# Query transfers, normalisation's end, local stage and both ends moved; dense products between global scores in a one-core transformer mixer layer

## What is computed

```python
xn = layernorm(x)
# attention: 16 heads of 16; 4 global (causal), 12 local (causal, 64 back)
q, k, v = split(xn @ w_qkv + b_qkv)
ctx = softmax(mask(q @ k.T * 0.25)) @ v
attn = ctx @ w_out + b_out
# two branches of 8 experts of rank 64, on Q, K and on Q @ W_inv.T, K @ W_inv.T
prod = (Q @ V) * cumsum(K @ W)
weights = softmax(gelu(Q @ router_w1.T + router_b1) @ router_w2.T + router_b2 + expert_bias)
branch = ((prod * weights) @ U + weights @ b) / position
ffn = (fwd + alpha * inv) @ W_O.T
out = x + attn + ffn
```

## Time and profile before

| | us |
|---|---|
| median of 3 runs | 1456.86 (1455.05 to 1458.92) |
| the profiled execution: its own time | 1456.11 |
| its span, first to last instruction | 1454.4 |
| TensorE busy (matmul) | 1356.6 (93%) |
| VectorE busy | 1012.4 (70%) |
| ScalarE busy | 774.1 (53%) |
| GpSimd busy | 581.9 (40%) |

### The profile page before, as it was taken

One profiled execution on the slowest core, in us unless ns is written; L12 is line 12 of the kernel. 1 busy time (PEld: TensorE's weight loads), 2 busy tenths in 40 slices (PEclk: granted clock), 3 DMA queues, 4 the chain that ended last, 5 costly groups with the idle time before them and its releaser, 6 DMA issues.

```text
span 1454.4 us, 35948 instructions
## 1 busy us (share of the span) xinstructions
PE 1356.6 (93%) x14481; PEld 1031.0 (71%) x14481; DVE 1012.4 (70%) x2082; ACT 774.1 (53%) x1368; POOL 581.9 (40%) x663
## 2 busy tenths in 40 slices
PE   5888999999999999999999999999999999999986
PEld 4567685777858777686867868587775878678773
DVE  6667877568756887568775777567885678757661
ACT  3334537464564636655374644647356463845544
POOL 2034343453424444354434535254442534345350
PEclk9999999999999999999999999999999999999997
DMA  8530625416172542617253171624517163441710
GB/s 184 126 95 23 168 69 136 116 60 175 41 170 69 128 128 73 153 32 179 76 129 110 57 188 29 170 83 110 146 43 181 34 154 102 118 121 42 185 34 16
DMA packets 184279, 154.45 MB, mean 106 GB/s; under 512 B 37554, under 2 KB 183857, under 8 KB 184113
## 3 DMA queue, kind: packets, MB, share of 16 engines
q1 hardware_dynamic: 184112, 152.16, 40.8%
HBM read 108.57 MB, written 37.22 MB: 100 GB/s over the span
## 4 chain that ended last, share of the span: by engine, by line
PE 66%; DVE 10%; ACT 8%; issue 6%; DMA 5%; POOL 3%; SPq 2%; ACTq 0%; POOLq 0%; DVEq 0%
PE PS L699 34%; PE PS L811 11%; PE PS L847 4%; ACT HE L1092 3%; PE PS L906 3%; PE PS L892 3%; DMA rest<-weights_d 2%; ACT HE L1084 2%; PE PS L924 2%; PE PS L833 2%; PE PS L989 2%; PE PS L935 2%; DMA weights_d<-weights_t 2%; PE PS L867 2%; DVE tok L1191 1%
## 5 line engine op out<-in xcount | busy, mean ns | idle before, releaser
L1540 POOL TENSOR_TENSOR PL<-prod,PH 128x512 fp32r<-128x512 f32 x128 | 167.4, 1308 | 180.6 <-ACT PH L1066 180.3
L1535 POOL TENSOR_TENSOR prod<-prod,rest 128x512 f32<-128x512 f32 x96 | 123.2, 1283 | 263.5 <-DMA rest<-weights_d 183.0
L1066 ACT ACTIVATE PH<-prod 128x512 fp32r<-128x512 f32 x128 | 80.8, 631 | 264.4 <-DVE prod L1340 264.4
L699 PE MATMUL PS<-XH,WH 128*128 128x512 f32 x512 | 216.9, 424 | 4.5 <-DVE rest L1209 1.8
L1264 DVE TENSOR_REDUCE block_peak<-PS 128x4 f32<-128x512 f32 x288 | 179.8, 685 | 49.0 <-PE PS L847 48.9
L699 PE MATMUL PS<-XH,WL 128*128 128x512 f32 x512 | 203.4, 397 | 0.0
L699 PE MATMUL PS<-XL,WH 128*128 128x512 f32 x512 | 203.1, 397 | 0.0
L1092 ACT ACTIVATE HE<-PS 128x512 f32<-128x512 f32 (+1 forms) x320 | 159.9, 552 | 34.3 <-PE PS L906 31.4
L1517 POOL TENSOR_SCALAR_AFFINE_SELECT HE<-HE 128x256 f32<-128x256 f32 x128 | 51.2, 406 | 287.2 <-ACT HE L1092 283.7
L1340 DVE TENSOR_TENSOR prod<-PS,prod 128x512 f32<-128x512 f32 x128 | 87.7, 685 | 94.5 <-PE PS L699 73.1
L811 PE MATMUL PS<-UH,PH 128*128 128x256 f32 x512 | 134.9, 296 | 0.0
(11 more groups left out here) (190 smaller groups left out, 3046.2 us busy)
## 6 DMA issues: line engine op xcount, KB each, us to landing
parts_d<-area SPq DMA_DIRECT2D x32, 768.0 KB, 5.0
area<-parts_d SPq DMA_DIRECT2D x128, 192.0 KB, 5.9
rest<-weights_d SPq DMA_DIRECT2D x192, 128.0 KB, 3.6
area<-parts_d SPq DMA_DIRECT2D x32, 576.0 KB, 5.7
tok<-in_L_attn_x_dram SPq DMA_DIRECT2D x16, 512.0 KB, 6.2
xt<-in_L_attn_x_dram SPq DMA_DIRECT2D x16, 512.0 KB, 4.7
wide<-weights_d SPq DMA_DIRECT2D x64, 128.0 KB, 3.5
out_dram<-xt SPq DMA_DIRECT2D x16, 512.0 KB, 4.1
```

Of the source, the lines that this page charges most:

```text
L699: ins = e.matmul(ps, a, b, start=first and k == 0, stop=last and k == n - 1, skip_group_check=True)
L1066: e.activation(PH[:, h, :], prod[:, j % 3, :], ACT.Copy).then_inc(phi)
L1535: e.tensor_tensor(prod[:, j % 3, :], prod[:, j % 3, :], wide[j % WIDE], ALU.mult).then_inc(weighed)
L1540: e.tensor_tensor(PL[:, j % 2, :], prod[:, j % 3, :], PH[:, j % 2, :].bitcast(F32), ALU.subtract).then_inc(plo)
```

## The change

All of it is in the order of the stages, in who does two sets of memsets, and in how one stage is cut:

- **Dense between scores.** In a global block the side work now stands between the first and the second score (in the last block behind both), and then comes the `gav` of the block before. `norm` pieces are hung on the value groups.
- **Local stage.** Both `turn`s come ahead of the first scores; `parts` start one group earlier; `hidden 0` moves into the sixth group.
- **Norm's end in parts.** "scale" is no longer a piece of `norm`: it is four stages of one operation each, behind peak blocks 2 to 5 (for chunk 1: all four behind the last peak group). `tok_done` counts four per chunk.
- **Query transfers.** The four are cut 3 + 1 around the transfer of `wide 0`, in place of 2 + 2.
- **Both ends.** `consts`' memsets of SBUF go into `boot`, the first stage, still on DVE. `settle` moves from DVE to POOL, with its waits. In the last chunk the expert work left over starts behind the first local group, and `finish` 15 0 stands in the middle of the global stage, not behind its first block.

```diff
-    NORM = (... "correct", "square", "correct", "scale")
+    NORM = (... "correct", "square", "correct")
...
     def global_groups(ch):
-        order = []
         tl = tiles(ch % NC)
-        for n, (j, half) in enumerate(tl):
-            order.append([(add_gscore, ch, j, half, pair) for pair in range(2)])
-            if n:
-                order.append([(add_gav, ch, *tl[n - 1])])
-        return order + [[(add_gav, ch, *tl[-1])]]
+        scores = [[[(add_gscore, ch, j, half, pair)] for pair in range(2)] for j, half in tl]
+        return scores, [[(add_gav, ch, j, half)] for j, half in tl]
...
         if ch == 0:
             add_norm(1, order)
+            for t in range(T):
+                order[-1].append((add, "scale", 1, t))
...
         run(experts[0] + peaks[0])
         if ch and nxt:
-            add("norm", ch + 1, len(NORM) - 1)
+            for t in range(T):
+                peaks[2 + t].append((add, "scale", ch + 1, t))
         weave(experts[1:split], peaks[1:])
...
         if nxt:
-            side = [[(add_turn, ch + 1, 0), (add_turn, ch + 1, 1)] + last_mix, [(add_rows, ch, 1)]]
-            side += [[(add_parts, ch + 1, w, b)] for w in (1, 0) for b in range(DB)]
-            side[-1] += [(add, "sums", ch + 1, k) for k in range(DB)]
+            for k in range(DB):
+                add_turn(ch + 1, k)
+            side = [last_mix] + [[(add_parts, ch + 1, w, b)] for w in (1, 0) for b in range(DB)]
+            side[1].append((add_rows, ch, 1))
+            side += [[(add_hidden, ch + 1, 0)] + [(add, "sums", ch + 1, k) for k in range(DB)]]
...
-            side = [[(add_rows, ch, 1)]] + experts[split:] + [last_mix]
+            side = experts[split:] + [last_mix]
+            side[0] = side[0] + [(add_rows, ch, 1)]
         weave(local_groups(ch), side)
...
-            for j in range(2 * DB):
+            for j in range(1, 2 * DB):
                 add_hidden(ch + 1, j)
...
+        last, done = len(scores) - 1, 0
+        for n in range(1, last + 1):
+            upto = -(-len(side) * n // last)
+            between = [stage for group in side[done:upto] for stage in group]
+            done = upto
+            first, second = scores[n]
+            run(first + (second + between if n == last else between + second) + values[n - 1])
+        run(values[last])
...
@@ vector_program, "boot" (moved here from "consts")
+                    for c in range(NC):
+                        e.memset(block_peak[c][:, :, :, :], LOWEST)
+                    q.step(e.memset(peak[:, :, :], 0.0))
+                    for view, value in ((ones1, 1.0), (wslots[:, :, :], 0.0), (Va[:, :, :, :], 1.0)):
+                        ins = e.memset(view, value)
+                    ins.then_inc(readied)
...
@@ vector_program
-                    else:
-                        for t in range(T):
-                            ins = e.tensor_scalar(tok[:, t, :], tok[:, t, :], mv[:, t, 0:1], var[:, 3, t:t + 1], ALU.subtract, ALU.mult)
-                        ins.then_inc(tok_done)
+                elif kind == "scale":
+                    ch, t = key
+                    q.wait_step()
+                    e.tensor_scalar(tok[:, t, :], tok[:, t, :], mv[:, t, 0:1], var[:, 3, t:t + 1], ALU.subtract, ALU.mult).then_inc(tok_done)
...
@@ gpsimd_program (in vector_program it had no waits, and is gone there)
+                elif kind == "settle":
+                    q.wait_ge(fold_ps, product_nth("fold", 5, 1))
+                    q.wait_ge(out_lo, 1)
+                    for view in (WT[G16:KSTK, :], KL[G16:KSTK, :, WINDOW:], KG[G16:KSTK, :, :]):
+                        e.memset(view, 1.0).then_inc(ones_set)
+                    q.wait_ge(ones_set, 3)
...
@@ sync_program, "stacks"
-                        for rows, i in STACK if half is None else STACK[2 * half:2 * half + 2]:
+                        for rows, i in STACK if half is None else (STACK[:3], STACK[3:])[half]:
```

More of the change, by code:

```diff
@@ L151, in peak_use @@
         return f"bank{(4, 5, 6, 7)[turns['peak'] % 4]}"
-    NORM = ("moments", "start", "square", "correct", "square", "correct", "square", "correct", "scale")
+    NORM = ("moments", "start", "square", "correct", "square", "correct", "square", "correct")
     def add_lpeak(ch, t, grp, bank):
@@ L322, in add_norm @@
         at_ = len(order) // 3
-        steps = len(NORM) - (1 if ch > 1 else 0)
-        for n in range(steps):
-            order[at_ + n * (len(order) - at_) // steps].append((add, "norm", ch, n))
+        for n in range(len(NORM)):
+            order[at_ + n * (len(order) - at_) // len(NORM)].append((add, "norm", ch, n))
     def peak_groups(ch):
@@ L352, in mixer_layer @@
         add("norm", 0, n)
+    for t in range(T):
+        add("scale", 0, t)
     add("split_qkv")
@@ L434, in mixer_layer @@
             add("stacks", ch + 1, "local")
-            for j in range(2 * DB):
+            for j in range(1, 2 * DB):
                 add_hidden(ch + 1, j)
-        order = global_groups(ch)
-        side = []
+        scores, values = global_groups(ch)
         if nxt:
             first_x, first_c = ([(add, ch + 1, 0, part) for part in range(2)] for add in (add_x, add_c))
-            run(first_x + order[0] + first_c)
+            run(first_x + scores[0][0] + scores[0][1] + first_c)
             add("logits", ch + 1, uses=["bank7"])
             add("chigh", ch, 0)
-            order = order[1:]
             if ch + 2 < CHUNKS:
[L447 to L450, removed]
+                add_norm(ch + 2, values)
+            side = [[(add_gates, ch + 1), (add, "crest", ch, 0)], [(add_gate_parts, ch + 1)]] + [[]] * (2 * (ch % NC))
+            side += [[(add_values, ch + 1, 0)], [(add_values, ch + 1, 1)], [(add_finish, ch, 0)]]
         else:
+            run(scores[0][0] + scores[0][1])
             add("crest", ch, 0)
-        side.append([(add_finish, ch, 0)])
-        weave(order, side)
+            side = [[], [(add_finish, ch, 0)]]
+        last, done = len(scores) - 1, 0
[6 more added lines that the diff above has]
+        run(values[last])
         if nxt:
@@ L713, in tensor_program @@
                         q.wait_ge(selected, 2)
-                    q.wait_ge(tok_done, ch + 1)
+                    q.wait_ge(tok_done, T * (ch + 1))
                     take(i, *stage)
@@ L1168, in vector_program @@
                         q.wait_ge(x_in, 16 * (ch + 1))
-                        q.wait_ge(tok_done, ch)
+                        q.wait_ge(tok_done, T * ch)
                         for t in range(T):
@@ L1233, in vector_program @@
                     e.tensor_tensor(p3, left, p2, ALU.subtract).then_inc(part3)
-                elif kind == "settle":
-                    for view in (KL[G16:KSTK, :, WINDOW:], KG[G16:KSTK, :, :], WT[G16:KSTK, :]):
-                        e.memset(view, 1.0).then_inc(ones_set)
                 elif kind == "keep":
@@ L1387, in vector_program @@
                 elif kind == "consts":
-                    for c in range(NC):
-                        e.memset(block_peak[c][:, :, :, :], LOWEST)
-                    q.step(e.memset(peak[:, :, :], 0.0))
-                    for view, value in ((ones1, 1.0), (wslots[:, :, :], 0.0), (Va[:, :, :, :], 1.0)):
-                        ins = e.memset(view, value)
-                    ins.then_inc(readied)
                     q.wait_ge(selected, N_SELECT)
```

## The result

| | before | changed |
|---|---|---|
| median of the runs, us | 1457.89 (4 runs, 1455.05 to 1462.80) | 1439.14 (4 runs, 1437.22 to 1442.25) |
| profiled execution: own time, span | 1456.11, 1454.4 | 1440.78, 1439.1 |
| PE, DVE, ACT, POOL busy | 1356.6, 1012.4, 774.1, 581.9 | 1354.2, 987.6, 773.4, 595.0 |

The ratio is 0.9869, with a 95% interval of 0.9844 to 0.9894: 1.3% faster, 15.3 us between the two spans. The lines of the changed kernel stand 9 to 13 lines further down: L776 is now L785, L833 is L842, L867 is L876, L699 is L708; the scalings' L1191 is L1208.

A forecast was written before the change was run, and what follows sets the result against it. PE was taken as the bound, computing 1356.6 of 1454.4 us, with many small waits left to win. The terms summed to -24.0, taking 1456.1 to 1432, with a range of 1420 to 1447.

The forecast's parts named there:

- right: Success signs: POOL's memsets 9 to 14 us; PE waits: L1077's mask under 4 us, `open` under 5, queries under 4.
- wrong: Failure signs: new PE waits for DVE in odd chunks; global scores waiting for exps over 15 us; query wait unchanged.
- `consts`, -1.7: Start: memsets move into DVE's idle time in `boot`, PE's 2.52 us wait partly won; bounds 0 and -2.5.
- `settle`, -2.8: Start: memsets leave DVE for POOL, PE's 3.04 us wait for the gate transpose falls; bounds -2.2 and -3.0.
- Chunk 0, -1.0: Four scalings come behind `found`, taking 1.38 us for 2.49 ahead of a product PE awaits; bounds 0 and -3.1.
- Local stage, -6: Dense work in the second group covers mask waits of 9.6 us; 0.4 us in 15 chunks; bounds 0 and -9.6.
- Odd front, -9: Gates-to-`open` chain: 1.05 us sooner in 8 chunks (-8.4), scalings -2.5, landing against issue +1.9; bounds -2.5 and -18.5.
- the third query ahead of `wide` 0 costs 0: Odd front: it would push `wide` 0 back by 0.3 us, covered by PE's 1.04 us of waiting; size 0.
- Scalings, -2.5 and +1.5 in the peak blocks: -2.5: 0.5 us in each of five odd fronts; +1.5: scalings delaying maxima or products, 0.2 us in seven odd chunks.
- the port rival: Odd chunks: each of 28 scalings meets a POOL multiplication, 21 us come back, no change at 1453; chance 0.07.
- Dense between scores, 0: Global blocks: first exp over early, second exp behind the `Va` copy; 0 net, bounds -4 and +6.
- Last chunk, -5: Last chunk: -3.5 from local-stage waits and slower clock, -1.5 from `finish` leaving the global front; bounds -2 and -8.

The follow-up runs named there:

- e8: e2 with the raw weights of `w_out` and U on two semaphores, and chunk 1's four scalings behind product 6 of chunk 0: 1430.69 us, ratio 0.9798.
- e5: Kernel before with the scalings' part of the change alone, four single operations behind peak blocks: 1444.45 us, ratio 0.9900.
- e12: Kernel before with the query transfers cut 3 + 1 around `wide` 0, nothing else: 1461.43 us, ratio 1.0020.
- e6: e2 with one step moved on VectorE alone, the transposition `ctx` 2 ahead of the queries' first `parts`: 1429.34 us, ratio 0.9793.
- e3: Changed kernel with `hidden` 0 back behind the local stage, all else kept: 1452.26 us, ratio 0.9964.
- e7: e2 with turns behind the first two scores, `mix` 7 split over two groups, `parts` and `hidden` 0 as before the change: 1436.56 us, ratio 0.9841.
- e2: Changed kernel with the query transfers cut 2 + 2 around `wide` 0, as before the change: 1431.40 us, ratio 0.9821.
- e4: Changed kernel with the old order of the global stage, `finish` 15 0 left in the middle: 1443.45 us, ratio 0.9887.
- e1: Changed kernel with the four scalings back in one set ahead of the expert stage, chunk 0's kept behind `found`: 1452.72 us, ratio 0.9953.

## Why the prediction was right, and which steps were not

It said 1432.0 with 1420 to 1447; the runs say 1439.1. In spans it was 24.0 to win, and 15.3 were won. Sign and range held, but not for the reasons given. Of its own signs, no wait at `open`, 0.2 us for L1077's masks and 9.2 us of memsets came as "right" had them; the wait for the queries came to 4.9 us, not under 4, and the new waits for products in odd chunks (3.7) were on its list for "wrong".

- **`consts`, -1.7: measured -0.4.** The 2.52 us went, and 2.56 for the last raw weights came, at 36.85 (before 37.23). The term let the second transfer land 4.6 us after its issue near 30.7, at 35.4; the chain that ended last has it under way for 6.0 (start us, us):

```profile
30.78 6.03 DMA ctok<-in_L_ffn_U_inv_dram
```

  The row was read rightly: in the kernel before the two took 4.5 and 4.8 us. What failed is that they would land as fast in the changed kernel. In all eleven profiles with the new start the second took 5.5 to 6.6 us, in all three with the old one 4.7 or 4.8; why, no run shows. In e8 the wait turned out needless: the two bias rows behind it read neither of the weights.
- **`settle`, -2.8: right.** PE's wait fell from 3.04 to 0.60, and POOL's memsets took 9.2 us by its rows (0.52 and 8.67), hidden. What both parts of the start gave is seen at A of chunk 0 when profiles with a like clock are compared. At full clock it stands at 82.4 with the old start and at 79.1 to 80.0 in five profiles with the new one; where the clock fell once ahead of it, at 83.4 and 83.6 (e5, e12) against 81.3 and 81.5 (the changed kernel, e6). So the start gave 2 to 3 us of the 4.5; the table shows 1.2, because there the first profile has full clock and the second has not.
- **Chunk 0, -1.0: wrong.** PE waits 3.27 us, 3.13 before. Behind `found` the set takes 1.38 us, as I took it to, which saves DVE 1.1. But a small piece of norm now stands between the last two maxima, and took 1.14 us there for the usual 0.16 (before, such a piece was stretched further ahead, where nobody waited):

```profile
117.29 1.14 DVE L1201 TENSOR_SCALAR var<-var 128x4 f32<-128x4 f32 x1
```

  e8 found the place that pays.
- **Local stage, -6: 0.** The masks' 9.6 us went to 0.2, as said. They came back as `hidden` 0's 10.6, which I had not looked for: its bank is freed by DVE behind some 3 us of `parts`. e3, e6 and e7 took that wait away in three ways, and each time another chain of the stage closed in: masks on POOL, then scores, exps and masks in a row, then the first value products. In the even chunks the orders of before, of the change, of e6 and of e7 end within 0.3 us of each other.
- **Odd front, -9: right in sum, by parts that came out otherwise.** E of the even to B of the odd chunks fell by 2.5 + 8.3 = 10.8. SP's order was costed at 0.63 us in each of 8 chunks, 5.0 of the term's 8.4; it lost 7.2 us in the middle (e2 against the changed kernel). The other 0.42 was the gates' exp: the gate weights do go out 0.7 us sooner ahead of E. The sentence that failed is that the third query ahead of `wide` 0 costs 0 because 1.04 us of PE's waiting cover it. Its issue does fit in SP's idle time, as said (e12). But the sentence looked at who waits for the queries, and not at whose data stand ahead of `wide` 0's on the way. The prediction had named landing against issue as its risk, at 1.9.
- **Scalings, -2.5 and +1.5 in the peak blocks: -13.7 (e5).** This is the term that was mis-sized most: 9.2 us came between A and B, where 8.7 of the wait at `open` went, and 4.8 from B to the local stage. I took 0.5 us for each of five chunks from the chain that ended last. In the row of chunk 7 and of chunk 1 the set stood 4.3 us on the way to `open`. Nor did I count what such a wait can do to the clock behind it. PE in the 10 us behind `open`, kernel before, chunks 1, 7 and 3 (us, PE busy, granted clock, DMA):

```profile
178.74:188.74 10.00, 9.87 (x88) 0.83 0.65 184
690.03:700.03 10.00, 9.87 (x88) 0.83 0.62 180
349.41:359.41 10.00, 9.66 (x92) 1.00 0.59 167
```

  Chunk 9 reads as 1 and 7 do, 5, 11 and 13 as 3 does. The three had waited 1.8 to 2.1 us at `open`, the four 1.1 to 1.3. A mean of 0.83 is a third of the stretch at 1.2 GHz and the rest at 2.4, and B to the local stage took 33.8 us in these three, 32.9 in the others: 2.7 of the 4.8. The changed kernel's stretches of chunks 1 and 7, from A on, which had no wait at `open`:

```profile
170.18:211.16 40.98, 39.90 (x380) 1.00 0.37 104
677.23:717.92 40.69, 39.72 (x382) 1.00 0.38 105
```

  The set took 1.38 to 4.32 us in the seven odd chunks of the kernel before. Cut in four and spread, 13 of 56 single scalings of the changed kernel are still stretched, to as much as 1.45 us for 0.40 (12 of 56 before). They take as long in all (34.7 us, 34.5 before), but PE hardly waits: the port rival's cost is refuted by e5, not because the stretch isn't there.
- **Dense between scores, 0: right** (e4, 0.9 us the other way, within the scatter). Its two sides cancel with queries 3 + 1. With 2 + 2 the gates' 0.7 us seem to come through (argued, not shown), since E to the next A is 29.0 in e2 against 34.0 in e5; no run undid that part alone there.
- **Last chunk, -5: -3.4.** The local stage took 2.4 us less, not 3.5, and for the most part not by its waits: those were 3.8 by the earlier trace rows and 0.5 for an exp, and are 3.7 (2.6 of them for POOL's masks). What went is the slow clock beside them, and with it 1.9 us of PE's busy time. The stage before and in the changed kernel:

```profile
1398.00:1419.20 21.20, 17.00 (x338) 0.92 0.02 4
```

```profile
1386.60:1405.40 18.80, 15.08 (x338) 1.00 0.02 3
```

  This is no chance: the three profiles with the old order of this stage (before, e5, e12) read 0.92 and 21.1 to 21.3 us, the eleven with the new one 1.00 and 18.8. Ahead of it, A to B took 0.6 us more. The global stage gave the 1.5, which is within what it scatters by (23.4 to 24.4 us with the old order, 22.9 to 24.1 with the new). PE's wait for `PL` went, and this came, 2.97 where 3.0 was said:

```profile
1408.98 1.10 PE L915 MATMUL PS<-area 99*128 99x256 bf16 x4 [2.97 <-ACT HE L1101]
```

So the middle's -13.5 met -12.3 by luck, by errors that cancel. Scalings: -1.0 said, -13.7 found (e5). The third query and SP's order: -3.1 said (8 x 0.63, and the 1.9 against it), +7.2 found. All the rest: -9.4 said (local stage 6.0, gates' exp 3.4), -5.8 found (e2 against e5), and not in the local stage: it lies in E to A (-5.0) and A to B (-2.4) behind the earlier gates and in B to D of the odd chunks (-1.5), with 1.0 lost in the even chunks and 2.2 in the global stage.

## What to carry to other kernels

Waits of an engine taken one by one mislead in a stage that several chains bound alike: measure the stage between two fixed instructions, and expect a removed wait to return as the next chain's. A transfer moved ahead of another costs its data's time as well as its issue; ask whose first use comes first, and put that one ahead. A wait can cost more than its own length, since PE's clock may fall behind it: in e5 8.7 us of waiting at `open` went and 13.7 us were won, 2.7 of them by the clock. And profiles of one kernel are to be compared stretch by stretch with the clock beside them; here the start alone moved by 2 us with it.

## What the runs showed of the hardware

- **The clock can fall behind short waits of an otherwise busy PE, and doesn't always.** In the kernel before, waits of 1.8 to 2.1 us at `open` were followed by 10 us at a mean of 0.83 in all three cases, waits of 1.1 to 1.3 by full clock in all four. Waits at `open` of 1.87 (e1), 1.91 (e12) and 1.56 us (e7, the first row) were followed by 0.83 too. But of fourteen equal waits of 1.66 us in e3's local stages only three were (the second row is behind one that wasn't, the third behind one that was), and after a wait of 2.0 us at A in e4 the clock stayed full. In e12 four falls stand behind two waits in a row, 1.0 to 1.1 us at A and 0.3 to 0.7 behind it.

```profile
1184.77:1194.77 10.00, 9.81 (x88) 0.83 0.62 184
```

```profile
226.81:236.81 10.00, 10.00 (x80) 1.00 0.54 156
314.56:324.56 10.00, 9.93 (x68) 0.83 0.54 155
```

  It isn't the wait alone in chunk 0 either, where a wait of 3.1 to 3.3 us was followed by three different clocks, in the kernel before, the changed one and e2:

```profile
118.00:130.00 12.00, 8.87 (x62) 0.86 0.02 3
```

```profile
118.00:130.00 12.00, 8.73 (x50) 0.72 0.01 2
```

```profile
118.00:130.00 12.00, 8.65 (x112) 1.00 0.02 3
```

  From A of chunk 0 to A of chunk 1 these three took 87.5, 88.9 and 86.5 us. That scatter is part of what separates two profiles of the same code there.
- **On one queue a transfer lands behind the data issued ahead of it.** Each further query transfer (192 KB) ahead of `wide` 0 (two of 128 KB) put its arrival back by 0.8, 1.2 and 0.3 us, while its issue moved by 0.1, 0.5 and 0.5. On the kernel before it was 1.2 for 0.1 (e12). The Trainium skill (DMA: Bandwidth & Descriptors, "Queues, rings and completion order") says that each DMA engine consumes a queue's descriptors in ring order; the two larger steps agree.
- **POOL fills memory as fast as DVE here.** `settle`'s 10752 bf16 elements took POOL 9.2 us (0.52 and 8.67); DVE took 5.18, 3.47 and 0.48 for the same three pieces. The 14 us that the prediction allowed for by POOL's one small memset were too many.
